# Constant rows and bias rows of batches 3 to 7 issued from GpSimd's queue, in an attention and quantized feed-forward kernel

## What is computed

```python
Q, K, V = (proj(Wq), proj(Wk), proj(Wv))              # 16 heads of 8
att = jnp.einsum('bhqd,bhkd->bhqk', Q, K) * (1.0 / math.sqrt(Dh))
att = att + b[0]
att = att * m + (1.0 - m) * NEG_INF                   # m: key mask
y = jnp.einsum('bhqk,bhkd->bhqd', jax.nn.softmax(att, axis=-1), V)
# feed-forward on y, position by position
h = jax.nn.silu(bit_linear(y, w_gate)) * bit_linear(y, w_up)
h = rms_norm(h, ln_weight)
x = x + bit_linear(h, w_down)
```

## Time and profile before

| | |
|---|---|
| time, median of 3 runs | 169.89 us (168.36 to 170.47) |
| the profiled execution | 169.71 us |
| its span in the trace | 167.9 us |
| TensorE busy / VectorE / ScalarE / GpSimd | 146.8 / 137.4 / 125.7 / 97.5 us |
| mean granted TensorE clock | 0.987 of full speed |

### The profile page before, as it was taken

How to read it: one execution, slowest core, us unless ns; L and a number is a source line. 1 busy time by engine, 2 the same in 40 slices (tenths; PEclk the granted TensorE clock), 3 DMA queues, 4 the chain that set the end, 5 groups by cost and what they waited for, 6 DMA issues and landing times.

```text
span 167.9 us, 4110 instructions
## 1 busy us (share of the span) xinstructions
PE 146.8 (87%) x1402; PEld 67.4 (40%) x1402; DVE 137.4 (82%) x205; ACT 125.7 (75%) x255; POOL 97.5 (58%) x175
## 2 busy tenths in 40 slices
PE   6989998999899899999599999988889755999682
PEld 2665643333333233333133343322222332665571
DVE  6789999788888788799677999893477799999961
ACT  3051469899799799889558889887899947998940
POOL 5889618539239239229849768821223667789900
PEclk9999999999999999999969999999999999999998
DMA  4975976245545344623323000000000000001121
GB/s 116 297 178 145 297 183 196 72 137 152 155 140 142 73 149 117 184 72 81 73 58 78 3 3 4 5 7 0 5 0 0 4 2 0 0 31 39 47 75 62
DMA packets 20124, 14.19 MB, mean 85 GB/s; under 512 B 2160, under 2 KB 19080, under 8 KB 20104
## 3 DMA queue, kind: packets, MB, share of 16 engines
q1 hardware_dynamic: 17480, 11.76, 24.5%
q10 hardware_dynamic: 2624, 2.17, 4.8%
HBM read 6.17 MB, written 1.07 MB: 43 GB/s over the span
## 4 chain that ended last, share of the span: by engine, by line
PE 36%; SPq 17%; ACT 14%; DVE 11%; issue 10%; POOL 7%; ACTq 2%; DMA 1%; DVEq 0%; POOLq 0%
SPq L263 11%; PE y_ps L1007 9%; PE s_ps L969 8%; ACT probs L523 4%; PE t_ps L987 4%; DVE hid L818 3%; ACT hid_sq L628 3%; PE y_ps L1048 2%; SPq L324 2%; DVE h_amax L833 2%; ACTq L263 2%; PE t_ps L954 2%; PE t_ps L945 2%; ACT h_T L645 2%; DVE maxes L882 1%
## 5 line engine op out<-in xcount | busy, mean ns | idle before, releaser
L882 DVE TENSOR_REDUCE maxes<-s_ps 128x4 f32<-128x1024 f32 x64 | 76.1, 1218 | 9.6 <-PE s_ps L969 9.4
L523 ACT ACTIVATE probs<-t_ps 128x512 f32<-128x512 f32 x128 | 70.9, 592 | 12.6 <-PE t_ps L987 11.5
L987 PE MATMUL t_ps<-q_st,k_st 64*128 64x256 bf16 x256 | 44.1, 276 | 5.7 <-ACT probs L523 3.0
L969 PE MATMUL s_ps<-k_st,q_st 64*128 64x256 bf16 x256 | 46.1, 276 | 0.2 <-DVE maxes L882 0.2
L1007 PE MATMUL y_ps<-probs,v_pad 128*18 128x256 f32 x512 | 39.5, 392 | 0.2 <-ACT probs L523 0.2
L969 PEld LDWEIGHTS s_ps<-k_st,q_st 64*128 64x128 bf16 x256 | 16.0, 94 | 29.3 <-issue 17.8
L411 POOL TENSOR_SCALAR nm_parts<-maxes 128x16 bf16<-128x16 f32 x16 | 3.3, 209 | 32.3 <-DVE maxes L882 28.6
L478 POOL TENSOR_TENSOR hw<-hid,ln_bc 128x512 f32<-128x512 f32 x8 | 10.2, 1272 | 17.0 <-DVE hid L807 9.9
L987 PEld LDWEIGHTS t_ps<-q_st,k_st 64*128 64x128 bf16 x256 | 14.2, 94 | 13.9 <-ACT probs L523 6.1
L1088 PE MATMUL s_ps<-w_q,ffn_x 128*128 128x512 bf16 x64 | 17.2, 380 | 2.5 <-DVE hid L818 2.3
L1007 PEld LDWEIGHTS y_ps<-probs,v_pad 128*18 128x18 f32 x512 | 9.7, 97 | 14.2 <-issue 12.2
(11 more groups left out here) (105 smaller groups left out, 230.2 us busy)
## 6 DMA issues: line engine op xcount, KB each, us to landing
q_st<-parts SPq DMA_DIRECT2D x48, 64.0 KB
k_st<-parts SPq DMA_DIRECT2D x33, 64.0 KB
w_f<-in_wgT ACTq DMA_DIRECT2D x2, 512.0 KB, 4.7
w_f<-in_wuT SPq DMA_DIRECT2D x2, 512.0 KB, 3.3
w_f<-in_wdT SPq DMA_DIRECT2D x2, 512.0 KB, 4.1
out<-o_sb SPq DMA_DIRECT2D x8, 128.0 KB, 1.7
k_st<-parts ACTq DMA_DIRECT2D x15, 64.0 KB
x_sb<-in_x SPq DMA_DIRECT2D x2, 256.0 KB, 4.5
```

What stands on the lines that cost most here:

```text
L523: act.activation(probs[:, t % NP_RING].rearrange("p e t -> p (e t)"), src, ACT.Exp, scale=SCALE)\
L882: dve.tensor_reduce(dst[:, :, s, :], s_ps[:, c % 2], AX.X, ALU.max).then_inc(s_maxed, 1)
L969: mm = pe.matmul(s_ps[:, c % 2, i, e, :], q_st[b % RING][rows, hp, qt * P:qt * P + P], k_st[b % RING][rows, hp, :], start=True, stop=True)
L987: mm = pe.matmul(t_ps[:, u % T_BANKS, e, :], k_st[b % RING][rows, hp, kt * P:kt * P + P], q_st[b % RING][rows, hp, :], start=True, stop=True)
```

## The change

- The constant rows and the bias rows of batches 3 to 7, ten DMAs, are issued from GpSimd's queue in steps 0 to 4, right behind `split_parts(n + 3)` and ahead of `negate_maxes(n + 1, 0)`. They tell of their landing on semaphores of their own, `later_rows_in`.
- The constant and bias rows of batches 0 to 2 stay on SP, with semaphores `first_rows_in`. Those of batch 2 are now issued together, so its bias rows go ahead of the maxima of batch 0.
- `stack_in` counts 12 DMAs in place of 14. TensorE waits for both semaphores at a batch's first score matmul.
- The two waits that kept a stack from being overwritten are now in `load_high`, in front of the parts, and in GpSimd's new function.
- Weight operation 0 goes from ahead of `negate_maxes(5, 0)` to behind it, in front of operation 1.

```diff
-LOADS = 2 * len(SPLITS) + 2
+LOADS = 2 * len(SPLITS)
...
         def load_high(queue, b, side):
+            if b >= RING:
+                queue.wait_ge(unit_ready, unit["t", 16 * (b - RING + 1) - 1] + 1)
+            elif b:
+                queue.wait_ge(q_zeroed, b + 1)
+                queue.wait_ge(k_zeroed, b + 1)
             queue.wait_ge(hi_ready, b + 1)
             load_part(queue, b, side, 0)
...
+                if n == -1:
+                    load_rows(2)
+                    load_bias(2)
                 if has(n + 3):
-                    load_rows(n + 3)
                     load_high(sp, n + 3, 0)
...
                 if has(n + 3):
-                    load_bias(n + 3)
                     load_low(sp, n + 3, (0, 1))
...
-            weight_steps = {4: ((0,), (1,)), 5: ((2, 3), (4, 5)), 6: ((6, 7), (8,))}
+            def load_constant_rows(b):
+
+                if b < RING:
+                    pool.wait_ge(q_zeroed, b + 1)
+                    pool.wait_ge(k_zeroed, b + 1)
+                    pool.dma_start(q_st[b % RING][BIAS_ROWS], ones6[:, :, :].to_broadcast([6, NHP, T]))\
+                        .then_inc(later_rows_in[b % RING], 16)
+                else:
+                    pool.wait_ge(unit_ready, unit["t", 16 * (b - RING + 1) - 1] + 1)
+                    pool.dma_start(q_st[b % RING][MAX_ROWS], zeros6[:, :, :].to_broadcast([6, NHP, T]))\
+                        .then_inc(later_rows_in[b % RING], 16)
+                pool.wait_ge(bias_stored, 16)
+                pool.dma_start(k_st[b % RING][BIAS_ROWS],
+                               bias_scr[b].rearrange("i k t -> (i k) t").unsqueeze(1).to_broadcast([6, NHP, T]))\
+                    .then_inc(later_rows_in[b % RING], 16)
+
+            weight_steps = {4: ((), (0, 1)), 5: ((2, 3), (4, 5)), 6: ((6, 7), (8,))}
             split_parts(1)
             for n in range(FIRST, LAST + 1):
                 if has(n):
                     negate_maxes(n, 1)
                 if has(n + 3):
                     split_parts(n + 3)
+                if n >= 0 and has(n + 3):
+                    load_constant_rows(n + 3)
                 for step in weight_steps.get(n, ((), ()))[0]:
                     quantize_weights(step)
```

More of the change, by code:

```diff
@@ L239, in adaln_ffn_kernel @@
         last_hm_done = sem("last_hm_done")
+        first_rows_in = [sem(f"first_rows_in{r}") for r in range(RING - 1)]
+        later_rows_in = [sem(f"later_rows_in{r}") for r in range(RING)]
         hT_ready = sem("hT_ready")
@@ L299, in load_rows @@
             def load_rows(b):
[L301 to L310, removed]
+                sp.wait_ge(q_zeroed, b + 1)
+                sp.wait_ge(k_zeroed, b + 1)
+                sp.wait_ge(small_const, 2)
+                sp.dma_start(q_st[b][BIAS_ROWS], ones6[:, :, :].to_broadcast([6, NHP, T])).then_inc(first_rows_in[b], 16)
             def load_bias(b):
@@ L315, in load_bias @@
                     sp.wait_ge(bias_stored, 16)
-                sp.dma_start(k_st[b % RING][BIAS_ROWS],
+                sp.dma_start(k_st[b][BIAS_ROWS],
                              bias_scr[b].rearrange("i k t -> (i k) t").unsqueeze(1).to_broadcast([6, NHP, T]))\
-                  .then_inc(stack_in[b % RING], 16)
+                  .then_inc(first_rows_in[b], 16)
             def load_max_rows(b, tau):
@@ L964, in scores @@
                         pe.wait_ge(stack_in[b % RING], 16 * LOADS * (b // RING + 1))
+                        if b < RING - 1:
+                            pe.wait_ge(first_rows_in[b], 32)
+                        else:
+                            pe.wait_ge(later_rows_in[b % RING], 32 * ((b + 1) // RING))
                     if c >= 2:
```

## The result

The changed kernel takes 168.09 us (median of 20 runs, 167.90 to 171.17), the kernel before 170.51 (median of 20, 168.36 to 173.42). The ratio is 0.9904, 95% interval 0.9877 to 0.9932: 1% faster, so within the 2% that was called no change, but on the other side from the forecast of 172.8. A ratio in this document leaves out, for each kernel, the executions in a slower state (over 1.5% above its fastest), so it can differ from the quotient of the medians, here 0.986. The profiled execution took 167.93 us with a span of 166.1, against 169.71 and 167.9.

What follows compares the result with a forecast made beforehand. Bound: three close engines, TensorE waiting on SP's late queue and on GpSimd in step 4. Stalls +3.91, step 4 +0.20, SP's gain -1.02, in all +3.1 us on 169.71: 172.8 us, range 166.3 to 179.0.

Steps and rivals of the forecast that it cites:

- What bounds the kernel: Late SP queue costs TensorE 1.02 us; L447 delays GpSimd's negation in step 4, a 1.81 us wait, then low clock, 1.52.
- D = 2.14: Time in us of GpSimd's two DMA issues ahead of the negation in steps 0 to 4, taken as 1.07 each.
- the stalls of steps 0 to 3: TensorE's new waits for GpSimd at k = 6: 1.72, 1.43, 1.20 and 0.76 us, counted as 3.91 after absorption.
- The rival of cheap issues: GpSimd's two issues take under 1.8 us together, giving 165.8 to 171.1 us; chance 0.30.
- The room: Slack before TensorE's k = 6 transpose waits for GpSimd's negation: 0.42, 0.71, 0.94, 1.38, 0.13 us in steps 0 to 4.
- I take 0.3 off each: Each k = 6 stall of steps 0 to 3 loses 0.3 us, absorbed because TensorE idles later for ScalarE anyway.
- 1.81 of wait cost 2.16: Step 4's TensorE wait lengthened its transpose interval by 2.16 us against 11.55, showing nearly all of a stall goes through.
- SP's gain of 1.02: Two fewer issues per step on SP end TensorE's two waits for the maxima, 0.52 and 0.50 us.
- no L987 waits for the landing of the maxima: Sign that the forecast is right: TensorE no longer idles for the row maxima's DMAs to land; no size given.
- The wait and the fall of the clock behind it stay: In step 4 the DMAs put back 2.14 us where moving L447 took away 1.94: +0.20, low clock remaining.
- Cover of the moved operation: Moved L447, 1.94 us, fits GpSimd's 2.53 idle; without a step 4 stall the negation of (5, 1) is up to 1 late.
- New waits for the rows' semaphores at no cost: TensorE's waits at a batch's first score matmul cost nothing: rows issued over 11.55 us ahead, landing takes 1.92.

Runs made afterwards that it cites:

- the relief run: Changed kernel with weight operation 0 back ahead of the negation and the ten DMAs of batches 3 to 7 left out on both queues: 168.23 us, ratio 0.9833.
- the run with the weight operation alone: Kernel before with only weight operation 0 moved behind the negation of (5, 0), all DMAs still on SP: 168.11 us, ratio 0.9807.
- the run at 2.25: Changed kernel with each GpSimd DMA cut in two over the heads, four issues per step ahead of the negation: 175.07 us, ratio 1.0347.
- the floor run: Changed kernel with the ten DMAs of batches 3 to 7 left out and weight operation 0 still moved: 165.40 us, ratio 0.9754.

## Why the prediction was wrong, point by point

- **What bounds the kernel:** right in kind. The late SP queue, the wait of 1.81 us in step 4 and its cause in L447 were read correctly; the relief run and the run with the weight operation alone show each as a gain of its own, 1.7% and 1.9%. The third cost, the low clock, is not in every execution (below).
- **D = 2.14 (the step that failed).** "Nearest is the issue of these same two transfers by SP [...] so I add the dispatch of one small operation": measured 1.21, and 1.41 for the first pair. SP's issue was not a lower neighbour; GpSimd's is shorter, and no dispatch comes on top. The whole sum hung on it, as it said. With 1.21 for 2.14 and every other term as forecast, the stalls of steps 0 to 3 fall from 3.91 to 0.69, step 4 gives 0.73 where it cost 0.20, and the 1.52 of the low clock comes back: 167.1 in place of 172.8. The profiled execution took 167.93; the 0.8 left is in the other terms, which follow. The rival of cheap issues named the case. Its 168.5 at D = 1.56 lies near the measured 168.09 partly by luck: its own sum at 1.21 gives the same 167.1. That the time stayed within 2%, to which the prediction gave 0.45, is no credit to the forecast: gains of 1.7% and 1.9% met a cost of GpSimd's issues of 2.7 to 3.0 us.
- **The room:** 0.42 and 0.13 in steps 0 and 4 held. The first pair took 32.12 - 30.71 = 1.41 against a wait of 0.98, so 0.43; step 4 had 1.22 - 1.04 = 0.18. In steps 1 and 2 it was 1.21 - 0.73 = 0.48 and 1.21 - 0.61 = 0.60, where 0.71 and 0.94 were taken: without SP's lateness TensorE arrives still earlier than its two waits say. The 0.42 of step 0 is not fixed: in the second profile of the changed kernel TensorE waited 1.42 us for the first maxima, and then only 0.26 there.
- **"I take 0.3 off each":** too much. In the relief run, without these waits, the first two intervals are 11.14 and 12.08; in the changed kernel they are 11.78 and 12.60. So waits of 0.73 and 0.61 cost 0.64 and 0.52, and about 0.1 is absorbed. At the transposes of step 3 the changed kernel is 1.75 us behind the relief run (70.71 against 68.96), where the rooms and the 0.3 make 0.69 at this D. At its own D the sum was therefore too low: 172.8 for 2.14, where the run at 2.25 took 175.07; there a second stretch of low clock and a longer one in step 4 add to it. Errors of opposite sign stood in the sum.
- **"1.81 of wait cost 2.16":** a wrong yardstick. The 11.55 is the interval from step 5 to 6. From step 3 to 4, with no wait in it, it is 81.05 - 69.21 = 11.84, so the wait cost 13.71 - 11.84 = 1.87.
- **SP's gain of 1.02:** mis-sized. With the DMAs left out it was 1.43 at the transposes of step 3, and 2.8 us in the timed runs. The prediction counted only the two visible waits and took their smallness as speaking against the change; SP's issue time was worth more than they show. The sign "no L987 waits for the landing of the maxima" did not come in full: the one of the first maxima, 0.74, is no lateness of SP's.
- **The clock.** "The wait and the fall of the clock behind it stay" was wrong with the wait's size: behind 1.04 us it did not fall. But the tie is looser than the prediction had it: behind 1.78 us in the second profile of before it did not fall either, and behind 1.74, 1.77, 1.81, 2.06 and 2.98 it did. So the length of the wait alone does not decide it, and what does is not shown. At D = 1.21 with a wait of 1.04 it held in both profiles.
- **Cover of the moved operation:** "up to 1 us late" for the negation of (5, 1), if no stall were left in step 4, did not come from the operation itself. In the floor run, with no stall and no issues, GpSimd still waited 0.23 us for VectorE before that negation, at 84.51. Only with the 1.19 us of issues behind the negation of (5, 0) as well did TensorE wait, 0.84.
- **New waits for the rows' semaphores at no cost:** held; no wait of TensorE for them is in the profile.

What stays open: why the gain of SP's relief in the timed runs, 2.8 us, is twice that of the profiles, 1.33 (169.71 and 168.38). In numbers the difference lies in the kernel before: its profiled execution is 1.34 us under the median of 171.05 in the relief run's set, that of the relief run 0.15 over its own. Long issues on SP, passed on by a queue without rest, late landings and the clock all differ between the two profiles of before. How much of the spread each makes was not measured.

## What to carry to other kernels

Before a DMA issue moves to another queue, look at what stands behind it there, and put it after the operation for which the in-order engine waits: with the ten DMAs on one side of five small operations the kernel took 168.1 us, on the other side 165.7. When a change has two edits, price each alone: here one line that moved no DMA reached the same median as both edits together. When the cost of an operation that the trace doesn't hold decides the sign, its nearest relative on another queue need not be a bound: SP's 0.78 was taken as a floor, and GpSimd's issue took 0.60.

## What the hardware showed that was not expected

- A DMA issue on GpSimd's queue occupied it for 0.54 to 0.62 us, the first one 0.81, for 24, 48 and 128 pieces of 512 bytes alike. The same issues of 48 pieces on SP took 0.75 to 0.81 in the kernel before. The first issue cost only 0.2 us more; the feared several us did not come.
- Issues on SP that take about 0.6 us now and then took longer: one took 1.68, and three together 2.74.
- The same wait of TensorE of 1.8 us was followed by 3.4 us at half clock in one execution of the kernel before and by none in another, while one of 1.74 was followed by 3.4 us and one of 2.06 by 6.8.
